# Exact bf16 parts in the first feed-forward network, and the second norm and router scores in one block by pairs of batches

## The reference

```python
xn = _layernorm(x); x = x + attention(xn) + ffn(xn)
```

## Time and profile before

| | |
|---|---|
| median of 3 runs | 2243.96 us (2239.49 to 2246.71) |
| the profiled execution's own time | 2245.6 us |
| its span, first to last instruction | 2243.8 us |
| mean granted clock of TensorE | 0.905 of 2.4 GHz |
| PE busy | 1871.0 us (83%) |
| DVE, ACT, POOL busy | 1632.1, 1197.4, 605.5 us |

### The profile page before, as it was taken

How to read it: one execution, slowest core, us unless ns; L and a number is a source line. 1 busy time by engine, 2 the same in 40 slices (tenths; PEclk the granted TensorE clock), 3 DMA queues, 4 the chain that set the end, 5 groups by cost and what they waited for, 6 DMA issues and landing times. The chain is left out here.

```text
span 2243.8 us, 45384 instructions
## 1 busy us (share of the span) xinstructions
PE 1871.0 (83%) x17688; PEld 991.0 (44%) x17688; DVE 1632.1 (73%) x2731; ACT 1197.4 (53%) x2431; POOL 605.5 (27%) x688
## 2 busy tenths in 40 slices
PE   2888887867546999999979899999789979887987
PEld 1222221443221335963333267776564434555755
DVE  5999999675788997569953945546566768966367
ACT  2999999433332886358866245556422420211465
POOL 1112110011684552124444633332124000000160
PEclk7899899987785999999989989999879989999986
DMA  8423420100362532733221122212012242430320
GB/s 280 86 57 80 85 64 1 76 18 6 101 195 50 126 58 73 212 77 66 48 33 45 45 65 67 64 50 76 10 33 73 86 126 87 138 93 13 113 57 34
DMA packets 156414, 172.01 MB, mean 77 GB/s; under 512 B 55308, under 2 KB 124886, under 8 KB 156194
## 3 DMA queue, kind: packets, MB, share of 16 engines
q1 hardware_dynamic: 142616, 144.18, 23.5%
q0 software_dynamic: 13584, 24.92, 4.5%
HBM read 95.73 MB, written 77.28 MB: 77 GB/s over the span
## 5 line engine op out<-in xcount | busy, mean ns | idle before, releaser
L443 ACT ACTIVATE a_E<-a_scores,a_nmax 128x512 f32<-128x512 f32 x512 | 343.7, 801 | 14.3 <-DVE a_nmax L376 13.1
L1022 ACT ACTIVATE a_E<-a_scores 128x512 f32<-128x512 f32 x512 | 273.6, 600 | 96.3 <-PE a_scores L1057 91.3
L376 DVE TENSOR_REDUCE a_nmax<-a_scores 128x2 f32<-128x1024 f32 x256 | 303.1, 1218 | 21.5 <-PE a_scores L458 17.6
L926 DVE TENSOR_REDUCE a_nmax<-a_first 128x2 f32<-128x1024 f32 x256 | 295.7, 1219 | 14.4 <-PE a_first L1047 13.3
L458 PE MATMUL a_scores<-a_Vh,a_Kh 48*128 48x512 bf16 x512 | 108.5, 422 | 95.1 <-ACT a_E L443 70.7
L1047 PE MATMUL a_first<-a_Kh,a_Qh 48*128 48x512 bf16 x512 | 147.5, 415 | 38.0 <-PEq L51 21.2
L471 PE MATMUL a_turn<-a_E,a_QS 128*32 128x256 f32 x2048 | 175.7, 420 | 2.3 <-DVE a_QS L386 1.8
L1057 PE MATMUL a_scores<-a_Qh,a_Kh 51*128 51x512 bf16 x512 | 161.0, 395 | 5.0 <-PEq L51 2.0
L1079 PE MATMUL a_out<-a_E,a_V 128*32 128x256 f32 x2048 | 162.1, 397 | 0.0
L443 ACT ACTIVATION_READ_ACCUMULATOR a_E<-a_scores,a_nmax 128x1 f32 x512 | 160.3, 321 | 0.0
L458 PEld LDWEIGHTS a_scores<-a_Vh,a_Kh 48*128 48x128 bf16 x512 | 24.9, 94 | 216.7 <-ACT a_E L443 176.3
(11 more groups left out here) (590 smaller groups left out, 4339.6 us busy)
## 6 DMA issues: line engine op xcount, KB each, us to landing
f_up<-in_L_up SPq DMA_DIRECT2D x32, 256.0 KB, 3.3
a_Kh<-a_rows_k SPq DMA_DIRECT2D x16, 384.0 KB, 6.2
a_Vh<-a_rows_v SPq DMA_DIRECT2D x16, 384.0 KB, 9.1
a_Qh<-a_rows_q SPq DMA_DIRECT2D x32, 192.0 KB, 4.3
a_Kh<-a_rows_k SPq DMA_DIRECT2D x32, 192.0 KB, 5.0
slots<-empty SPq DMA_DIRECT2D x8, 645.0 KB, 6.4
f_xe<-slots SPq DMA_DIRECT2D x40, 129.0 KB
outs<-zeros SPq DMA_DIRECT2D x8, 512.0 KB, 5.8
```

Source lines behind the costliest of these rows:

```text
L376: v.tensor_reduce(nmax[:, rd % 2, r1, :, q], bank(b, u)[:], AX.X, ALU.max, negate=True).then_inc(S["max_ready"], 1)
L443: m = a.activation(E[:, u % NE, x], bank(b, u)[:, x], ACT.Exp, bias=nmax[:, rd % 2, r1, x, q:q + 1], accum_out=Z[:, rd % 2, r1, x, q:q + 1])
L926: v.tensor_reduce(out, slot_bank(n)[:], AX.X, ALU.max, negate=True).then_inc(S["slot_read"], 1)
L1022: a.activation(E[:, u % NE, x], ps_s[n % 3][:], ACT.Exp, scale=SCALE).then_inc(S["exp_ready"], 1)
```

## The change

In f0, gate and up weights become bf16 (whole numbers up to 127, so exact), and the factor 1/127 moves into the sigmoid's scale and into the down weights. Each column of `g.XT` is split by POOL into three bf16 parts whose sum is the float32 value. A gate or up product becomes three bf16 products into the same PSUM bank. The parts of batches 0 and 1 are made in attention's main block, behind POOL's last work there; those of batches 2 to 7 in f0's block.

The stages ln1 and ln2 are dropped; layer 1's norm is done in the router's block. The mean of a normalised row is 0 and its sum of squares follows from the norm's own variance, so the second bn_stats goes away: the standard deviation and the Euclidean norm come from one product of two columns, and the mean's weight row is folded into the weights for x (`r1a` plus `r1m`/128), which leaves five statistics. SP issues six loads in place of five. All goes by pairs of batches, with a written order on every engine. The gelu's table is loaded early by an extra activation. `recycle_sems` is skipped where there is nothing to clear.

```diff
+FIRST_PARTS0 = 2
+def split_columns(pool, x, rest, parts):
+    pool.tensor_copy(parts[:, 0], x)
+    pool.drain()
+    pool.tensor_tensor(rest, x, parts[:, 0], ALU.subtract)
+    pool.drain()
+    pool.tensor_copy(parts[:, 1], rest)
+    pool.drain()
+    pool.tensor_tensor(rest, rest, parts[:, 1], ALU.subtract)
+    pool.drain()
+    return pool.tensor_copy(parts[:, 2], rest)
...
                     pool.tensor_copy(parts[:, 2], rest[:]).then_inc(S["parts_ready"], 1)
+                for b in range(FIRST_PARTS0):
+                    pool.drain()
+                    split_columns(pool, g.XT[:, b], rest[:, 0:T], g.f0_parts[:, b])
...
-                for n in range(3):
-                    m = v.tensor_scalar(wf[n][:], wf[n][:], float(np.float32(1.0 / 127.0)), None, ALU.mult)
-                m.then_inc(S["weights"], 1)
+                v.tensor_scalar(wf[2][:], wf[2][:], STEP ** 3, None, ALU.mult).then_inc(S["weights"], 1)
...
-                        a.activation(sig[:, n], ps_g[:, n], ACT.Sigmoid).then_inc(S["sig"], 1)
+                        a.activation(sig[:, n], ps_g[:, n], ACT.Sigmoid, scale=STEP).then_inc(S["sig"], 1)
...
+            @block.gpsimd
+            def _(pool):
+                for b in range(FIRST_PARTS0, NB):
+                    pool.drain()
+                    split_columns(pool, g.XT[:, b], rest[:], later[:, b - FIRST_PARTS0]).then_inc(S["parts"], 1)
...
-                    pe.matmul(ps_g[:, n], wf[0][:, n * 128:(n + 1) * 128], g.XT[:, b], start=True, stop=True)
-                    pe.matmul(ps_u[:, n], wf[1][:, n * 128:(n + 1) * 128], g.XT[:, b], start=True,
-                              stop=True).then_inc(S["gu"], 1)
+                    xp = g.f0_parts[:, b] if b < FIRST_PARTS0 else later[:, b - FIRST_PARTS0]
+                    if n == 0 and b >= FIRST_PARTS0:
+                        pe.wait_ge(S["parts"], b - FIRST_PARTS0 + 1)
+                    for ps, W in ((ps_g, wf[0]), (ps_u, wf[1])):
+                        for p in range(3):
+                            m = pe.matmul(ps[:, n], W[:, n * 128:(n + 1) * 128], xp[:, p], start=(p == 0), stop=(p == 2))
+                    m.then_inc(S["gu"], 1)
...
-                    for n in range(NT // 2):
-                        v.bn_stats(bst[:, n].rearrange("p s k -> p (s k)"), xn[:, 2 * n:2 * n + 2].rearrange("p s c -> p c s"))
...
+                    v.tensor_scalar(var[:, 0], moment, 1.0 / C, EPS, ALU.mult, ALU.add)
+                    v.tensor_copy(var[:, 1], moment).then_inc(S["var_ready"], 1)
+                    v.wait_ge(S["std_ready"], 1)
+                    v.reciprocal(rstd[:], std[:, 0]).then_inc(S["rstd_ready"], 1)
+                    v.drain()
+                    norm(0)
+                    norm(1)
+                    v.tensor_tensor(col(3), std[:, 1], rstd[:], ALU.mult)
+                    v.wait_ge(S["loaded"], 6 * 16)
+                    v.scalar_tensor_tensor(r1a[:], r1m[:], 1.0 / C, r1a[:], ALU.mult, ALU.add).then_inc(S["r1a_ready"], 1)
+                    v.drain()
+                    v.tensor_scalar(col(0), col(3), float((C - 1.0) ** -0.5), None, ALU.mult)
+                    for i in range(NG):
+                        extremes(i)
+                        if i + 1 < NG:
+                            norm(2 * i + 2)
+                            norm(2 * i + 3)
+                        near_zero(i)
+                        if i:
+                            take_logits(2 * i - 2)
+                            take_logits(2 * i - 1)
+                    take_logits(NB - 2)
+                    take_logits(NB - 1)
...
+                    a.activation(std[:], var[:], ACT.Sqrt).then_inc(S["std_ready"], 1)
+                    take_x(0)
+                    absolute(0)
+                    take_x(1)
+                    a.activation(g.unit_root[:], g.ident[:, 0:1], ACT.Gelu)
                     for i in range(NG):
...
+                        if i + 1 < NG:
+                            take_x(2 * i + 2)
+                            absolute(i + 1)
+                            take_x(2 * i + 3)
+                        features(2 * i)
+                        features(2 * i + 1)
+                        hidden(2 * i)
+                        hidden(2 * i + 1)
...
+                    turn_x(0)
+                    turn_x(1)
+                    pe.wait_ge(S["loaded"], 6 * 16)
+                    pe.wait_ge(S["r1a_ready"], 1)
+                    hidden(0)
+                    hidden(1)
+                    for i in range(NG):
+                        if i + 1 < NG:
+                            turn_x(2 * i + 2)
+                            turn_x(2 * i + 3)
+                        turn(2 * i)
+                        turn(2 * i + 1)
+                        add_features(2 * i)
+                        add_features(2 * i + 1)
+                        logits(2 * i)
+                        if i + 1 < NG:
+                            hidden(2 * i + 2)
+                        logits(2 * i + 1)
+                        if i + 1 < NG:
+                            hidden(2 * i + 3)
...
-STAGES = ("ln0", "a0", "f0", "ln1", "L1", "ln2", "L2", "L3")
+STAGES = ("ln0", "a0", "f0", "L1", "L2", "L3")
...
-            g.recycle_sems()
+            if g.sems:
+                g.recycle_sems()
```

More of the change, by code:

```diff
@@ L527, in ffn0 @@
     NH = 3
+    STEP = float(np.float32(1.0 / 127.0))
     ctx = ExitStack()
@@ L531, in ffn0 @@
         wi = g.f0_weights
-        wf = [k.sb(f"f0_wf{n}", [C, NH * 128]) for n in range(3)]
+        wf = [k.sb(f"f0_wf{n}", [C, NH * 128], BF16) for n in range(2)] + [k.sb("f0_wf2", [C, NH * 128])]
+        later = k.sb("f0_later_parts", [C, NB - FIRST_PARTS0, 3, T], BF16)
+        rest = k.sb("f0_rest", [C, T])
         sig = k.sb("f0_sig", [128, NH, T])
@@ L537, in ffn0 @@
         ps_o = [k.ps(f"f0_o{i}", [128, T]) for i in range(2)]
-        S = {n: g.sem(f"f0_{n}") for n in ("weights", "gu", "sig", "h", "out", "added")}
+        S = {n: g.sem(f"f0_{n}") for n in ("weights", "parts", "gu", "sig", "h", "out", "added")}
         with nc.Block(no_gpsimd_drain=True) as block:
@@ L1294, in col, with norm, extremes, near_zero @@
                         return stats[:, ts, n:n + 1].rearrange("p t o -> p (t o)")
[L1296 to L1307 removed]
+                    def norm(b):
+                        for r in range(R - 1):
+                            m = normalise(v, b, r)
+                        m.then_inc(S["xn_ready"], 1)
+                    def extremes(i):
                         ts = slice(i * GT, (i + 1) * GT)
                         v.drain()
[L1310 to L1311 removed]
+                        v.wait_ge(S["xn_last"], 2 * i + 2)
+                        v.tensor_reduce(col(1, ts), xn[:, ts], AX.X, ALU.min)
+                        v.tensor_reduce(col(2, ts), xn[:, ts], AX.X, ALU.max)
+                    def near_zero(i):
+                        ts = slice(i * GT, (i + 1) * GT)
                         v.wait_ge(S["abs_ready"], i + 1)
@@ L1316, in _, with take_logits @@
                         v.drain()
-                        v.tensor_scalar(col(5, ts), q[:, ts], 1.0 / C, None, ALU.mult).then_inc(S["stats_ready"], 1)
-                    for b in range(NB):
+                        v.tensor_scalar(col(4, ts), q[:, ts], 1.0 / C, None, ALU.mult).then_inc(S["stats_ready"], 1)
+                    def take_logits(b):
                         v.wait_ge(S["logits"], b + 1)
@@ L1321, in _, with take_x, absolute @@
                                       ).then_inc(S["logits_read"], 1)
+                    moment = g.stats[:, :, :, 2:3].rearrange("p n s o -> p (n s o)")
+                    v.tensor_scalar(var[:, 0], moment, 1.0 / C, EPS, ALU.mult, ALU.add)
[21 more added lines that the diff above has]
+                    take_logits(NB - 1)
+                @block.gpsimd
+                def _(pool):
+                    pool.wait_ge(S["rstd_ready"], 1)
+                    for b in range(NB):
+                        normalise(pool, b, R - 1).then_inc(S["xn_last"], 1)
                 @block.scalar
                 def _(a):
+                    def take_x(b):
+                        a.wait_ge(S["x_turned"], b + 1)
+                        a.activation(g.XT[:, b], ps_x[b % 2][:], ACT.Identity).then_inc(S["x_read"], 1)
+                    def absolute(i):
+                        a.wait_ge(S["xn_ready"], 2 * i + 2)
+                        a.wait_ge(S["xn_last"], 2 * i + 2)
+                        a.activation(tmp[:, i * GT:(i + 1) * GT], xn[:, i * GT:(i + 1) * GT], ACT.Abs).then_inc(S["abs_ready"], 1)
                     def features(b):
@@ L1375, in logits @@
                         m.then_inc(S["logits"], 1)
-                    pe.wait_ge(S["loaded"], 5 * 16)
-                    pe.wait_ge(S["roots"], 2)
-                    turn(0)
-                    for b in range(NB):
-                        if b + 1 < NB:
-                            turn(b + 1)
-                        hidden(b)
```

(6 more changed lines are left out.)

59 lines of the change are left out of this document (32 added, 27 removed).

## The result

| | before | after |
|---|---|---|
| median of 20 runs each | 2245.26 us (2238.13 to 2263.36) | 2235.35 us (2230.19 to 2244.57) |
| ratio, 95% interval | | 0.9948 [0.9931, 0.9965] |
| the profiled execution's own time | 2245.6 us | 2231.13 us |
| its span | 2243.8 us | 2229.3 us |

The change makes the kernel faster by 0.52%, or 11.7 us (7.9 to 15.5) of 2245.26. 2233.4 was forecast.

The account below looks back on a forecast made before the run. PE was taken to bound f0, DVE then PE's clock the norm and router. Gains 10.3 - 0.5 + 0.3 + 0.5 = 10.6 us from 2245.6 gave 2235.0, or 2233.4 as a median; range 2221 to 2243.

Parts of the forecast that it names:

- the clock going up and down: Norm and router block: PE's clock falls and returns in each pair; whole kernel gains 5 to 16 us, chance 0.65.
- f0: Stage f0: cheaper products and fewer weight scalings, less a slower start, gain 10.3 us, range 9 to 10.7.
- attention, beside the first parts: Attention: POOL's splits of batches 0 and 1 lengthen up to two of DVE's query scalings, costing 0.5 us.
- norm and router: Merged block: 12.0 us to first statistics, then pairs with the clock partly down; 56.1 us, 0.3 gained, range 51 to 61.
- step into layer 2: Barrier into layer 2: the empty stage's clearing goes, gaining 0.5 us of the 1.42 us DVE was idle.
- f0's products: f0: three bf16 products replace each float32 one, 48 products by 0.213 gain 10.2 us; batch period 6.55 us.
- The weights: f0's start: two of three scalings go, gaining 0.55 us; three casts stay, their new type costed at nothing.
- The 0.4 for DVE's longer third at the start: f0's start, before down products: DVE's 1.5 us a third exceeds PE's 1.3, costing about 0.4 us.
- the cold case: Router block with PE at 1.2 GHz all along: 65.1 us, 8.7 more than before.
- A clock held at 1.00: Rival, norm and router block: clock stays at 2.4 GHz, kernel gains 22.6 us, 2221.4; chance 0.15.
- A clock held at 0.50: Rival, router: clock stays at 1.2 GHz, kernel gains 1.6 us, 2242.4; chance 0.14.
- POOL as the bound: Rival, f0: POOL's splits set the stage, slower than before at 11 us a split; kernel 2287 at 16.6; chance 0.06.

Follow-up runs that it names:

- e5: Changed kernel, but in f0 POOL begins its splits only when the weights are scaled: f0 58.23 us in place of 59.32, one execution 2232.21 us.
- e7: Kernel before with f0's bf16 parts and the old norm and router order, features product padded to 128 rows: ratio to before 0.9938, median 2237.29 us.
- e6: Changed kernel with each of the six splits in f0 done twice: f0 70.70 us, one execution 2260.46 us.
- the repeat: The changed kernel run again without an edit, beside other runs on the same chip: ratio to before 0.9969 [0.9948, 0.9989], block 54.54 us.
- e3: Changed kernel with the product of the five statistics padded by zeros to 128 rows: 2224.0 us, ratio to before 0.9906, block 42.34 us.
- e11: Changed kernel padded to 128 rows, the added rows of the statistics holding ones in place of zeros: block 43.35 us, one execution 2224.65 us.
- e9: Padded changed kernel, with f0's POOL splits behind the weights and ACT taking absolute values earlier: 2218.71 us, ratio to before 0.9868, block 39.96 us.
- e10: Kernel of e9, with DVE waiting only for the two loads it folds, issued first: 2218.35 us, ratio to before 0.9869, block 39.23 us.
- e1: Kernel before with only f0's bf16 parts, norm and router as before: ratio to before 0.9961 [0.9940, 0.9982], f0 59.44 us.

## Why the prediction was right

The forecast was the clock going up and down, and a gain of 10.6 us. By its steps, in the profiled executions:

| step | forecast gain | measured |
|---|---|---|
| f0 | 10.3 | 9.66 (68.98 to 59.32) |
| attention, beside the first parts | -0.5 | about 0 |
| norm and router | 0.3 | -1.2; over all profiles, nothing that can be told |
| step into layer 2 | 0.5 | 0.36 |

**f0's products: right.** Six batches' periods fell by 1.26 each (7.83 to 6.57), and the first two batches together by 2.75 (12.10 from PE's first weights at 412.33 to the first down product at 424.43; 9.35 after). That is 10.3 us, against 10.2 for 48 products.

**The weights: this step failed.** I counted two scalings less, 0.55 won. The trace of after shows 0.66 lost: POOL's first split lengthens the three casts and the one scaling left. I had seen such lengthening in attention and priced it there, but not at f0's start, where POOL begins in the same instant. e5 settles it. The long scaling ends 0.22 us behind POOL's subtraction (414.35 and 414.13), and the long scaling of the queries below ends 0.08 behind one (312.90 and 312.82). The Trainium skill, "SBUF — State Buffer", section "SBUF: two separate sides", says that GpSimd and DVE, when DVE has two inputs there or runs in a faster mode, take a shared pair of ports as an exclusive lock for a whole instruction, while the other is blocked. The trace agrees for these two, in that each ended just behind POOL's instruction; in which mode the scaling of the weights ran, and which of the three casts waited, it doesn't show. POOL was held up too: its first cast and subtraction took 0.79 and 1.34 beside the weights, and 0.62 and 1.16 in the next split.

**The 0.4 for DVE's longer third at the start** did not show: the first two batches won 2.75, where 2 x 1.28 less 0.4 would be 2.2.

**Attention: nothing lost.** From the start of POOL's last old split to f0 it was 109.2 us before (301.19 to 410.40) and 109.0 after (302.82 to 411.81). One scaling of the queries took 0.80 beside the new splits; nothing of it reaches f0's start.

```profile
302.82 1.04 POOL L374 CAST a_parts_next<-a_KV_next 128x1024 bf16<-128x1024 f32 x1 [36.28 <-DVE a_KV_next L426]
...
311.66 1.16 POOL L193 TENSOR_TENSOR a_rest_next<-XT,f_first_parts 128x512 f32<-128x512 f32 x1
...
312.10 0.80 DVE L405 TENSOR_TENSOR a_QS<-a_QT,a_rZ 128x64 f32<-128x64 f32 x1
```

A split took 4.86 in place of 4.2, so f0's last ended at 441.2 and not 435.6, with no wait of PE.

**Norm and router: the mechanism was right, the place of the cold stretches was not.** DVE's wait was 1.54 where 2.5 was forecast, and the first statistics stood at 11.3, not 12.0. Then the four pairs took, forecast and measured: 11.05 and 12.87, 13.2 and 11.63, 13.2 and 12.39, 6.7 and 9.74 (482.42, 495.29, 506.92, 519.31, 529.05). I let only the second half of three pairs be at 1.2 GHz. In fact the first and the last pair were so whole, and each middle pair had 3.4 us at 2.4 GHz. The 15.1 of a middle pair at 1.2 GHz less these 3.4 is the 11.7 that the second took; PE's wait for ACT in it, which I had counted with 1.1, was 0.50 at most, I take it because the slower transposes leave ACT time. What was forecast for pairs at 1.2 GHz all along, 13.1 for the first and 9.4 for the last, is what they took (12.87, and 9.74 with the step into the next block): the prices were right, and where the clock would be down was not. These misses go against each other, which is luck, and the sum came to 57.9 for 56.1, inside the 51 to 61. By the forecast's own end, the last copy of logits, it is 57.5.

**Slips in the working.** The terms given for a middle pair add to 9.3 at most, not 9.45, and those of the cold case to 64.7, not 65.1; neither moves the forecast by half a microsecond. A POOL 2.3 times slower is where f0 loses all its gain; by the same rule POOL begins to set f0 at some 1.9 times.

The rule weighed there (the Trainium skill, "TensorE: Matmul & The Clock Gate", section "Part 4: PE-mode transpose": full rate doesn't engage for transposes) is contradicted by e7 as well, in the row shown there: up to the rise at 477.55 PE had done nothing in this stage but transposes, from 471.74 on, and was then granted 1.00.

**The rivals.** A clock held at 1.00 (2221.4) is what padding makes of this kernel: 2224.0. A clock held at 0.50 was not seen in any profile. POOL as the bound was tried by e6, and comes where the rule puts it.

**The sum.** The steps give 9.66 - 1.2 + 0.36, or 8.8 us; the median fell by 9.9 and the ratio gives 11.7 (7.9 to 15.5), in the repeat 7.0 (2.5 to 11.7). All agree. That the median came within 2 us of 2233.4 is luck in part: the steps were off by -0.6, 0.5, -1.5 and -0.1, and the same gain was 11.7 us in one measurement and 7.0 in the other. The two profiled executions differ by 14.5 us in their span: 1.4 were lost ahead of f0 and 7.5 won behind the block, of which only 0.36 has a cause that I can name.

## What to carry to other kernels

When an engine has a clock that follows its work, the shape and the order of small products can decide the price of the big ones beside them: here padding a 5-row product with zeros to 128 rows cost 1.1 us of clearing and took a block from 55 to 42 us. Look at the stretches of granted clock in a block before reordering it; a better order with the clock down was worth nothing that could be told, and some 6 to 8 us with the clock up. Padding is no rule for every order: the old one held 1.00 with 6-row products once it was there. Where work is handed to POOL, look at what DVE does in that same instant, and let POOL start behind it if it has slack.

## What the runs showed of the hardware that was not expected

- The padding to 128 rows adds no instruction on PE, and its clock stays at 1.00: 33.7 us in e3, 28.8 in e11, 25.8 in e7, 32.0 in e9, 34.0 in e10, up to the block's end each time. From the first padded product on it did not fall in any of them. With 5 rows it fell within the block in each of six profiles of the merged order, and with 64 it fell in the one there is. Yet the old order held 1.00 with 6 rows, for 20.0 us before and 23.7 in e1. What in the product the chip responds to is not settled by these runs.
- Code that no edit touched wanders between executions. A stretch of layer 3, from one DVE instruction to another, took 122.39 us in the profile of after and 131.10 in that of e6, at nearly the same clock and with nearly the same busy time of DVE:

```profile
1905.33:2027.72 122.39, 100.16 (x3179) 64.79 (x3177) 100.21 (x159) 29.67 (x56) 2.92 (x3) 0.96 0.37 106
```

```profile
1917.83:2048.93 131.10, 104.47 (x3180) 66.31 (x3178) 100.40 (x160) 29.66 (x56) 2.92 (x3) 0.95 0.36 99
```

The time from the block's end to the end of the run was 1698 to 1719 us over all profiles here, in no order with the edits. Its cause stays open. It is why one profiled execution can't judge a change of 10 us in this kernel, while a stretch that wanders less than the change can: f0 with its parts took 59.1 to 60.1 us over eight profiles, the block with 5 rows 52.9 to 57.9 over six.
